# The last three stages of a six-stage transformer kernel in one block, each stage's opening moved beside the end of the stage before

## What is computed

```
x = x + 0.5 * expert_ffn(layernorm(x))        # f1
x = x + dilated_attention(layernorm(x))       # a1
x = x + 0.5 * expert_ffn(layernorm(x))        # f2
x = x + 0.5 * channel_mix(layernorm(x))       # c1
x = x + batch_attention(layernorm(x))         # b1
x = x + 0.5 * channel_mix(layernorm(x))       # c2
```

```
xr = mu_r * x + (1 - mu_r) * x_prev;  xk = mu_k * x + (1 - mu_k) * x_prev
out = sigmoid(xr @ W_r.T) * (square(relu(xk @ W_k.T)) @ W_v.T)
```

```
q, k, v = x @ Wq.T, x @ Wk.T, x @ Wv.T
scores = q @ k.reshape(b, d, s) / 16
attn = softmax(scores, axis=0)                # over the batch
out = where(tril, attn, 1e-9) @ v
```

## Time and profile before

| | us |
|---|---|
| runs | 4073.08, 4068.54, 4068.47 |
| median | 4068.54 |
| profiled execution | 4073.62 |
| its span, first to last instruction | 4071.8 |
| c1, first load to last output of VectorE | 3332.9 to 3520.0 |
| b1 | 3524.5 to 3877.1 |
| c2 | 3880.8 to end |
| TensorE busy | 3827.8 (94%) |
| VectorE busy | 3206.5 (79%) |
| ScalarE busy | 3070.9 (75%) |
| GpSimd busy | 2279.0 (56%) |

### The profile page before, as it was taken

The page is one execution under the profiler, slowest core; times in us unless marked ns, Lnnn a source line. Parts: engine busy times, 40 slices in busy tenths (PEclk is TensorE's granted clock), DMA queues, the critical chain, the costliest instruction groups (busy, mean ns, idle before and its releaser), DMA issues. The chain is left out here.

```text
span 4071.8 us, 82459 instructions
## 1 busy us (share of the span) xinstructions
PE 3827.8 (94%) x29464; PEld 3347.3 (82%) x29464; DVE 3206.5 (79%) x7740; ACT 3070.9 (75%) x7818; POOL 2279.0 (56%) x1818
## 2 busy tenths in 40 slices
PE   7999999999889999999997899999999979899979
PEld 6888888888778888888886788888888868798868
DVE  7888888888667878787875888888888868656567
ACT  6888888888678888888885788888888868432066
POOL 7888888888511111111100888888888857311356
PEclk8999999999999999999998899999999989899989
DMA  2000000000100000000001100000000013321532
GB/s 65 16 17 16 17 16 17 17 17 19 42 13 12 23 12 23 12 23 12 23 7 49 32 16 21 17 17 17 17 17 17 14 43 93 102 95 54 157 111 89
DMA packets 135065, 141.99 MB, mean 35 GB/s; under 512 B 8672, under 2 KB 131968, under 8 KB 134656
## 3 DMA queue, kind: packets, MB, share of 16 engines
q1 hardware_dynamic: 134656, 136.71, 10.6%
HBM read 80.06 MB, written 56.62 MB: 34 GB/s over the span
## 5 line engine op out<-in xcount | busy, mean ns | idle before, releaser
L296 POOL TENSOR_TENSOR f_grid<-f_sim 128x1024 f32<-128x1024 f32 x512 | 968.6, 1908 | 0.0
L1423 ACT ACTIVATE a_ex<-a_p_s,a_mneg 128x128 f32<-128x128 f32 x2048 | 726.4, 408 | 149.6 <-DVE a_mneg L1477 149.6
L682 DVE SCALAR_TENSOR_TENSOR f_p_u<-f_grid,f_te,f_p_dot 128x1024 f32<-128x1024 f32 x512 | 652.9, 1275 | 113.3 <-PE f_p_dot L106 66.8
L304 POOL TENSOR_TENSOR f_q<-f_q 128x1024 f32<-128x1024 f32 x256 | 607.2, 2382 | 122.4 <-ACT f_q L554 120.0
L691 DVE SCALAR_TENSOR_TENSOR f_q<-f_p_u,f_rz,f_grid 128x1024 f32<-128x1024 f32 x512 | 650.6, 1271 | 0.4
L535 ACT ACTIVATE f_grid<-f_grid,f_negm 128x1024 f32<-128x1024 f32 x512 | 559.5, 1144 | 0.0
L1423 ACT ACTIVATION_READ_ACCUMULATOR a_ex<-a_p_s,a_mneg 128x1 f32 x2048 | 507.2, 248 | 0.0
L439 PE MATMUL f_p_y<-f_eup,f_wT 128*128 128x256 f32 x2048 | 472.9, 379 | 0.0
L434 PE MATMUL f_p_y<-f_wdn,f_hs 128*128 128x256 f32 x2048 | 468.3, 382 | 0.0
L439 PEld LDWEIGHTS f_p_y<-f_eup,f_wT 128*128 128x128 f32 x2048 | 388.7, 190 | 57.5
L434 PEld LDWEIGHTS f_p_y<-f_wdn,f_hs 128*128 128x128 f32 x2048 | 378.9, 190 | 49.5
(11 more groups left out here) (622 smaller groups left out, 10460.9 us busy)
## 6 DMA issues: line engine op xcount, KB each, us to landing
x_f<-f_yt SPq DMA_DIRECT2D x64, 256.0 KB, 2.2
f_xt<-x SPq DMA_DIRECT2D x32, 256.0 KB, 2.9
a_xt<-x_f SPq DMA_DIRECT2D x16, 512.0 KB, 3.8
x_a<-a_yt SPq DMA_DIRECT2D x16, 512.0 KB, 2.9
f_xt<-x_a SPq DMA_DIRECT2D x32, 256.0 KB, 2.9
c_xt<-x_f SPq DMA_DIRECT2D x16, 512.0 KB, 4.6
x_c<-c_yt SPq DMA_DIRECT2D x16, 512.0 KB, 3.1
b1p_xt<-x_c SPq DMA_DIRECT2D x16, 512.0 KB, 3.9
```

Of the source, the lines that this page charges most:

```text
L296: g_grid.mark(pool.tensor_tensor(grid[v][:, hd, :].rearrange("p (i j) -> p i j", i=XROWS), sx[:, hd, :].unsqueeze(2).to_broadcast([P, XROW ...
L304: g_pair.mark(pool.tensor_tensor(q[v][:, 2 * k, :], q[v][:, 2 * k, :], q[v][:, 2 * k + 1, :], ALU.add), f"{v}{k}")
L682: d_mask.mark(dve.scalar_tensor_tensor(out=p_u[:], in0=grid[v][:, hd, :], scalar=te[:, v, hd, TOP - 1:TOP], in1=p_dot[:], op0=ALU.is_ge, o ...
L1423: last = act.activation(ex[t.step % 2][:, i, n, :], p_s[i][:, n, :], ACT.Exp, bias=mneg[:, i, n:n + 1], accum_out=z[t.step % 2][:, i, n:n ...
```

## The change

The last three stages become three objects (`Stage`) whose parts are functions; `mix_and_attend` opens one block and calls them in turn for each engine. The semaphores of all three are allotted together and not cleared in between. The SBUF buffers of a stage are allotted as before from the same base, so those of the three lie over one another; their order is changed so that what the next stage writes first lies where the one before has read last already, and waits guard the rest (`keys_read`, `done`, `all_stored`, `scores_read`, `outputs_read`, `stored`).

The order of each engine's instructions at the two seams is new:

- SyncE issues the DMAs of b1's opening before the store of row 14 of c1, and c2's weights after group 17 of b1 and its first five rows among the groups 23 to 27. A row is loaded once its store has landed (`stored`).
- TensorE transposes b1's row 0 before `values(15)` of c1, and c2's row 0 after group 28 of b1.
- VectorE opens b1 (statistics, scaling, low part of the first weight and of row 0, statistics of row 1) before `output(15)` of c1; c2's opening stands among the groups 18 to 31.
- GpSimd makes the roots of c2's rows 0 and 1 among its `gather`.
- ScalarE runs the stages one after another; in the mixing stages the cast of the first weight now stands before `scale(0)`.
- In b1 `key(0)` stands before the transposes of row 1, the raw weights are loaded into `q_blk` in place of `k_all`, and the last 16 groups have another order.

```diff
-def channel_mix(nc, name, src, dst, w):
+def channel_mix(nc, sems, name, src, dst, w, prior=None):
...
+        def load(sp, n):
+            if prior:
+                prior.stored(sp, n)
+            sp.dma_start(xt[n % RING][:], row_tiles(src, at_(n))).then_inc(s_ld[n % RING].sem, 16)
...
+        def sync(sp, after=None):
+            for n in range(B):
+                if after and n == B - 2:
+                    after.open_sync(sp)
+                d_out.wait(sp, at_(n), "y")
+                sp.dma_start(row_tiles(dst, at_(n)), yt[n % 2][:]).then_inc(s_st[n % 2].sem, 16)
+                if n + RING < B:
+                    load(sp, n + RING)
+            for k in range(2):
+                sp.wait_ge(s_st[k].sem, 16 * (B // 2))
...
+        def tensor(pe, after=None):
+            turn_h(pe, 1)
+            for n in range(B):
+                keys(pe, n)
+                if n:
+                    values(pe, n - 1)
+                receptance(pe, n)
+                if n + 2 < B:
+                    turn_h(pe, n + 2)
+            if after:
+                after.open_tensor(pe)
+            values(pe, B - 1)
...
+            weight(0, wk)
+            scale(0)
...
+        def open_vector(dve):
+            clear(dve)
+            front(dve, 0)
+            rests(dve)
+            weight(dve, 0)
+            front(dve, 1)
+            mixed(dve, 0)
+            weight(dve, 1)
+
+        def vector(dve, after=None):
+            front(dve, 2)
+            for n in range(B):
...
+                if n:
+                    output(dve, n - 1)
+            if after:
+                after.open_vector(dve)
+            output(dve, B - 1)
...
-def batch_attention(nc, name, src, dst, w):
+def batch_attention(nc, sems, name, src, dst, w, prior):
...
-        raw = [k_all[:, B - 1 - n, :, 0:D] for n in range(3)]
+        raw = [q_blk[:, B - 2 * (n + 1):B - 2 * n].rearrange("p a c s -> p a (c s)") for n in range(3)]
...
-        groups = [(qb, g) for qb in reversed(range(NB)) for g in range(G)]
+        groups = [(qb, g) for qb in (3, 2) for g in range(G)] + [(1, g) for g in range(5)] + [
+            (0, 0), (0, 1), (1, 5), (0, 2), (0, 3), (1, 6), (0, 4), (0, 5), (1, 7), (0, 6), (0, 7)]
...
+        def stored(sp, row):
+            n = group_of[0, row // GB]
+            sp.wait_ge(s_y[n % 2], 16 * (n // 2 + 1))
...
+            put(range(12, 18))
+            t_s.wait(sp, at_(last_of[0]))
+            after.load_weights(sp)
+            put(range(18, 24))
+            after.load(sp, 0)
+            after.load(sp, 1)
+            put(range(24, 25))
+            after.load(sp, 2)
+            after.load(sp, 3)
+            put(range(25, 27))
+            after.load(sp, 4)
+            put(range(27, NB * G))
...
+            for n in range(B):
+                query(n)
+                if n == 0:
+                    key(n)
+                if n + 1 < B:
+                    turn_h(pe, n + 1)
+                if n:
+                    key(n)
+                if n < B - LATE:
+                    value(n)
...
+            outputs(range(16, 29))
+            after.turn_h(pe, 0)
+            outputs(range(29, NB * G))
...
+                if n == 0:
+                    prior.keys_read(act)
+                if n == 1:
+                    prior.done(act)
+                if n == B - 2:
+                    prior.all_stored(act)
+                a_hT.mark(act.copy(hT[n][0][:], p_tr))
...
+            gather(1, range(0, 6))
+            after.ready(pool)
+            after.root(pool, 0)
+            gather(1, range(6, 7))
+            after.root(pool, 1)
+            gather(1, range(7, G))
...
+        def open_vector(dve):
+            dve.memset(unseen[:], UNSEEN).then_inc(s_z, 1)
+            dve.memset(half[:], -0.5).then_inc(s_z, 1)
+            statistics(dve, 0)
+            scale(dve, 0)
+            weight(dve, 0, wq)
+            turned(dve, 0)
+            statistics(dve, 1)
+
+        def vector(dve, after):
+            weight(dve, 1, wk)
+            scale(dve, 1)
+            weight(dve, 2, wv)
...
+            output(range(16, 18))
+            after.clear(dve)
+            output(range(18, 26))
+            after.rests(dve)
+            after.front(dve, 0)
+            output(range(26, 28))
+            after.weight(dve, 0)
+            after.front(dve, 1)
+            output(range(28, 30))
+            after.mixed(dve, 0)
+            output(range(30, NB * G))
+            after.weight(dve, 1)
...
+def mix_and_attend(nc, src, dst, w):
+
+    with ExitStack() as sems:
+        x_c, x_b = (nc.dram_tensor(f"x_{k}", (N, D), F32, kind="Internal").ap() for k in ("c1", "b1"))
+        c1 = channel_mix(nc, sems, "c1", src, x_c, w)
+        b1 = batch_attention(nc, sems, "b1", x_c, x_b, w, c1)
+        c2 = channel_mix(nc, sems, "c2", x_b, dst, w, b1)
+        with nc.Block() as block:
+            @block.sync
+            def _(sp):
+                c1.open_sync(sp)
+                c1.sync(sp, b1)
+                b1.sync(sp, c2)
+                c2.sync(sp)
...
```

More of the change, by code:

```diff
@@ new lines, in values, with open_tensor @@
+        def values(pe, n):
+            if n == 0:
+                pe.wait_ge(s_w, 16 * 3)
+            d_ks.wait(pe, at_(n))
+            if n:
+                d_out.wait(pe, at_(n - 1), "rk")
+            for v in range(T):
+                for c in range(DC):
+                    last = pe.matmul(p_v[:, v, :], ks[n % 2][:, c, v * P:(v + 1) * P], wv[:, c, :],
+                                     start=c == 0, stop=c == DC - 1)
+            t_v.mark(last)
+        def open_tensor(pe):
+            turn_h(pe, 0)
@@ new lines, in clear, with front, rests @@
+        def clear(dve):
+            dve.memset(half[:], -0.5).then_inc(s_z, 1)
+            for x in range(2):
+                dve.memset(old[x][:, :, 0:1], 0.0).then_inc(s_z, 1)
+        def front(dve, n):
+            slot_wait(dve, s_ld, at_(n))
+            if n >= 2:
+                a_h.wait(dve, at_(n - 2))
+            norm.statistics(dve, at_(n))
+        def rests(dve):
+            dve.wait_ge(s_mu, 32)
+            dve.tensor_scalar(rest[:], mu[:], -1.0, 1.0, ALU.mult, ALU.add).then_inc(s_z, 2)
@@ new lines, in channel_mix @@
+    stage.load, stage.load_weights, stage.stored, stage.all_stored = load, load_weights, stored, all_stored
+    stage.root, stage.ready, stage.turn_h, stage.clear, stage.front, stage.rests = root, ready, turn_h, clear, front, rests
+    stage.weight, stage.mixed, stage.done = weight, mixed, done
+    stage.keys_read, stage.receptance_read, stage.values_read = keys_read, receptance_read, values_read
+    stage.open_sync, stage.open_gpsimd, stage.open_tensor, stage.open_vector = open_sync, open_gpsimd, open_tensor, open_vector
@@ L1055 @@
+    stage.sync, stage.gpsimd, stage.tensor, stage.scalar, stage.vector = sync, gpsimd, tensor, scalar, vector
+    return stage
 MH, HD = 16, D // 16
@@ new lines, in turn_h, with open_tensor, scores_read @@
+        def turn_h(pe, n):
+            norm.d_h.wait(pe, at_(n))
+            if n:
+                d_hT.wait(pe, at_(n - 1))
+            for v in range(NB):
+                for c in range(DC):
+                    last = pe.transpose(p_tr[:, c, v * P:(v + 1) * P], h[:, v, c * P:(c + 1) * P], ident[:])
+            t_hT.mark(last)
+        def open_tensor(pe):
+            pe.wait_ge(s_id, 16)
+            turn_h(pe, 0)
+        def scores_read(e):
+            d_sub.wait(e, at_(len(blocks) - 1))
```

1081 lines of the change are left out of this document (522 added, 559 removed).

## The result

| | before | after |
|---|---|---|
| median of 4 runs, us | 4069.64 | 4040.43 |
| lowest, highest | 4068.47, 4073.08 | 4039.57, 4043.09 |
| span of the profiled execution | 4071.8 | 4037.8 |

The ratio is 0.9928, 95% interval 0.9911 to 0.9945: 29.2 us faster where 28.5 were forecast.

The account below looks back on a forecast made before the run. TensorE bounds the steady rows, so only the seams can gain: 4073.6 - 13.5 - 15.0 = 4045.1 us profiled, and with the median's 5.1 lower carried over, 4040 us; range 4032 to 4050.

Parts of the forecast that it names:

- The bound and the place of the gain: Steady mixing rows: TensorE busy 124.5 of 125.0 us, untouched by the change; only time at the two seams can move.
- fourth rival: Both seams: a SyncE wait prevents early opening; only two block ends go, 4.5 us each, giving 4059.5; chance 0.04.
- Seam 1: c1 to b1: the opening runs beside c1's end, so `query(1)` comes earlier; gain taken 13.5 us, bounds 10 and 16.
- The clock at seam 1: TensorE's 5.0 us gap, c1 to b1: a clock fall costs transposes 0.9, `values(15)` 2.4 us more; gain 12.9, otherwise 14.4.
- two gaps: Old trace, TensorE idle: 2.4 GHz kept 5.3 us after c1's last matmul, 1.2 GHz reached 3.0 us after b1's.
- The first rival: c1 to b1: TensorE falls to 1.2 GHz and stays through `query(0)`; that seam gives 10 us, time 4043.5; chance 0.15.
- Seam 2: b1 to c2: c2's opening runs among b1's last outputs, `keys(0)` earlier by 15.2, taken as 15 us; bounds 10 and 19.7.
- the weights' cost on the `xo` ring: b1 to c2: c2's weight loads, issued after group 17, make groups 20 and later come 2 us late.
- Rival 2: b1 to c2: c2's early rows hold up the `xo` loads and outputs; that seam gives 5 us, time 4050; chance 0.13.
- Rival 5: Steady rows of both mixing stages: new buffer addresses slow VectorE; at 30% slower 33 us lost, time 4073; chance 0.03.
- The swap on ScalarE: Mixing stages: the first weight's cast before `scale(0)` makes that 0.4 us late; between 0.4 lost and 0.4 gained, zero taken.
- The carrying over of 5.1 us: Whole kernel: the timed median lay 5.1 us below the profiled execution, so 4045.1 became a forecast of 4040.

Follow-up runs that it names:

- e1_serial: Changed kernel, still one block, but both openings put behind the ends of the stages in front on every engine; 4066.85 us, ratio 0.9981.
- e3_seam2: Changed kernel with the c1-to-b1 seam made serial and only the b1-to-c2 seam overlapped; 4052.79 us, ratio 0.9951.
- e2_seam1: Changed kernel with the b1-to-c2 seam made serial and only the c1-to-b1 seam overlapped; 4055.87 us, ratio 0.9952.
- e13_again: The changed kernel itself, unedited, timed and profiled again beside later versions on the same chip; 4044.06 us, ratio 0.9925.
- e10_key: Changed kernel with `values(15)` before b1's transposes and b1's key weight cast and its low part made earlier; 4040.69 us, ratio 0.9920.
- e4_values: Changed kernel with TensorE doing `values(15)` of c1 before b1's first transposes; 4039.89 us, ratio 0.9919.
- e6_weights: Changed kernel with c2's weights issued ahead of the stores of b1's groups 16 and 17; 4037.07 us, ratio 0.9914.
- e9_swap: Changed kernel with ScalarE doing `scale(0)` before the cast of the first weight again; 4044.89 us, ratio 0.9928.

## Why the prediction was right, step by step

- **The bound and the place of the gain.** Right. Steady rows and the middle of b1 have the durations they had; all of the change's 29.3 us is at the seams. From R to K it is 361.0 us where it was 388.0. The forecast had 359.4 for 388.1, counted from 3513.84, which is the start of `values(15)`; the last `receptance` ends at 3514.00. e1_serial prices the ends of blocks by themselves: 3.4 and 4.0 us (2.5 and 4.8 in e3_seam2 and e2_seam1), where the prediction's fourth rival had 4.5 each.
- **Seam 1.** Taken 13.5, measured 14.0 here and 13.1 in e13_again. Against R: the transposes forecast at 4.9 (4.7 measured), `query(0)` 9.5 (10.3), `key(0)` 13.5 (13.8), `query(1)` 20.2 (20.5), the wait for row 2 1.7 (1.54).
- **The clock at seam 1.** Left open between two levels, and the lower one came in all the profiles with this order. It cost less than the 3.3 us put on it. In this profile `values(15)` took 4.1 us, not 6.0, since the clock was back 2.8 us after the transposes began, and `query(0)` ran at full clock; in the other five with this order `values(15)` took 4.8 to 5.6 us. That gives 1.4 us here and 2.9 at most. Of the two gaps that the prediction held against each other it misread one: a mean of 0.72 in the earlier trace rows between the levels 1 and 0.5 puts the fall at 3522.4, 5.0 us after the last matmul and not 5.3. Nothing of the sum hangs on it. The first rival, a low clock through `query(0)`, is false for this kernel, and it is what the other order brings (e10_key). The advice of the Trainium skill, "TensorE: Matmul & The Clock Gate", section "Why this matters for your kernels", against idle gaps between bursts is borne out by half. Closing the 4.7 us gap gained 0.9 to 2.3 us (e4_values), but the clock fell all the same, behind gaps of 1.28 and 2.41 us.
- **Seam 2.** Taken 15, measured 15.3 to the last yt, by two errors that cancel. K came 12.9 us earlier, not 15.2. That the two nearly cancel is luck. The term that failed is the weights' cost on the `xo` ring, put at 2 us: group 20's output is at M + 22.6, and at M + 18.8 both in the kernel before and in e6_weights, so the cost is 3.8 (2.8 in e9_swap), and e6_weights takes 3.2 of it back at K. The statistics of row 0, forecast at M + 32.8, came at 34.5, and group 27, forecast at 39.8, at 43.0. The sum also has a slip of 0.4: 3861.6 and 2 us are 3863.6, not 3863.2. What the forecast left out is the clock behind K: it priced the start of `keys(0)`, and TensorE, which is now busy with outputs just before, runs it in 3.0 us instead of 5.5. The spread of the last eight outputs was forecast at 19 and is 20.3.
- **Rival 2, contention,** is true in kind and small in size: `xo` lands after 3.8 us, not 2.8, groups 20 and 27 wait 5.1 and 4.0 us, and the seam still gives 15, not 5. The Trainium skill, "DMA: Bandwidth & Descriptors", section "Issuing engines are not separate DMA queues", has all DMAs run on the same 16 engines and interleave. These waits agree.
- **Rival 5, new addresses.** False: VectorE is busy 105.2 us in 125, not more.
- **The swap on ScalarE.** Put at nothing, with `scale(0)` 0.4 us late. It came 1.5 us late after c1's first load (9.4 for 7.9), and c1's first store 0.5 (e9_swap).
- **The sum.** 28.5 forecast, 29.2 in the times. The carrying over of 5.1 us between the profiled execution and the median was sound: the mark ahead of c1 moves by up to 6.8 us between profiles of the same stages, and the profiled execution of the kernel after, at 4039.7, lies 0.7 below its median and not 5 above.

## What to carry to other kernels

At a seam between stages, first price the block's end by itself (here 2.5 to 4.8 us), then the opening that can run beside the tail (here 10 to 11 us more). Loads issued early were not free among work paced by loads: c2's weights cost 3.2 us among outputs that wait for their input. Issued 13 us sooner they cost nothing that shows: groups 18 to 24 come at the same times after M as in the kernel before, within 0.2 us. When an item on a critical chain is moved and nothing is gained, look at the granted clock of what follows it before looking for another queue.

## What the runs showed of the hardware

- The fall of TensorE's clock is not tied to a gap alone, and its place moves between profiles of the same order. In the six with an idle gap of 4.73 us after R it fell 2.6 (e2_seam1) to 5.1 us (e9_swap) after R, in two of them when work had begun again. It stayed low for 3.4 us in three of the six and for 6.8 in the others, which have the latest `query(1)` (21.5, 21.5 and 22.0). With gaps of 1.28 and 2.41 us it fell 1.4 us after work had begun again, and stayed low for 3.4 us (e10_key).
- The same kernel in two executions, after and e13_again, differs in the middle of b1: the time from the first maximum to the last is 145.6 and 147.1 us. Among the profiles the values lie at 145.6 to 145.7 (the kernel before, the kernel after and five of the experiments) or at 147.1 to 147.4 (seven experiments). A dip of the clock in the first half of that stretch is in the one and not in the other. The rows are those of the kernel after and then of e13_again, the same part of b1:

```profile
3706.80:3730.80 24.00, 21.51 (x134) 19.69 (x133) 18.65 (x28) 5.25 (x9) 6.71 (x2) 1.00 0.20 61
```

```profile
3710.00:3734.00 24.00, 21.50 (x124) 19.41 (x123) 18.28 (x27) 5.26 (x9) 6.71 (x2) 0.93 0.19 57
```

What decides between them stays open; it is 1.4 to 1.7 us that no order of instructions here explains.
